# Cross attention with image tokens, batch 15: image-score copies and the small columns of six head pairs move from DVE to ACT

## What is computed

```
q, k, v     = heads(x @ W_q), heads(text @ W_k), heads(text @ W_v)
probs       = softmax(q k^T / sqrt(8))                  over 124 text tokens
text_out    = probs v
qsem        = l2norm(probs @ text)                      width 256
fused       = q k_ip^T / sqrt(8) + 0.5 * qsem . l2norm(image)     4 image tokens
ip_out      = (softmax(fused) * mask) v_ip
out         = (text_out + ip_out) @ W_out + b_out + x
```

## Time and profile before

| | |
|---|---|
| Median of 3 runs | 218.13 us (216.04 to 218.46) |
| Profiled execution, its own time | 217.86 us |
| Its span, first to last instruction | 215.8 us |
| Granted TensorE clock | 1.000 |
| PE busy | 204.6 us (95%) |
| DVE busy | 181.1 us (84%) |
| ACT busy | 169.1 us (78%) |
| POOL busy | 149.7 us (69%) |

### The profile page before, as it was taken

The page is one execution under the profiler, slowest core; times in us unless marked ns, Lnnn a source line. Parts: engine busy times, 40 slices in busy tenths (PEclk is TensorE's granted clock), DMA queues, the critical chain, the costliest instruction groups (busy, mean ns, idle before and its releaser), DMA issues.

```text
span 215.8 us, 6904 instructions
## 1 busy us (share of the span) xinstructions
PE 204.6 (95%) x1589; PEld 191.5 (89%) x1589; DVE 181.1 (84%) x1147; ACT 169.1 (78%) x554; POOL 149.7 (69%) x255
## 2 busy tenths in 40 slices
PE   8898959999997999999999999999999999998984
PEld 8777959999996999999999999999999999987973
DVE  4547758998977798997979797989979798989893
ACT  2639949897986888897988888888969888887721
POOL 2165007379794979879696969698796969697870
PEclk9999999999999999999999999999999999999999
DMA  5524443837364462747365554647364656433101
GB/s 132 146 83 105 109 122 64 225 77 237 58 174 122 120 185 56 208 109 210 95 186 122 163 140 130 170 88 213 68 205 100 189 120 171 94 92 103 46 5 46
DMA packets 41580, 27.45 MB, mean 127 GB/s; under 512 B 8513, under 2 KB 39898, under 8 KB 41562
## 3 DMA queue, kind: packets, MB, share of 16 engines
q1 hardware_dynamic: 40922, 26.81, 47.5%
q10 hardware_dynamic: 640, 0.43, 0.8%
HBM read 10.06 MB, written 1.43 MB: 53 GB/s over the span
## 4 chain that ended last, share of the span: by engine, by line
PE 77%; DVE 5%; POOL 4%; DMA 4%; SPq 4%; ACT 3%; issue 2%; POOLq 0%; DVEq 0%
PE main_ps L974 14%; PE main_ps L976 14%; PE probsT_ps L956 13%; PE pa L946 9%; PE score_ps L1010 7%; DMA k_split<-kip_d 4%; PE pb L1038 4%; PE pb L1050 3%; PE pa L1066 3%; SPq L385 2%; PE main_ps L891 2%; PE pa L1058 2%; POOL rnorm L511 2%; PE pa L886 2%; DVE junk L734 2%
## 5 line engine op out<-in xcount | busy, mean ns | idle before, releaser
L629 ACT ACTIVATE probs<-score_ps,negmax 128x124 f32<-128x124 f32 x320 | 92.5, 401 | 2.0 <-DVE negmax L799 1.9
L734 DVE CUSTOM_DVE_ANT_0 junk<-main_ps,probs 128x124 f32<-128x124 f32 x320 | 77.8, 280 | 2.3 <-PE main_ps L976 2.1
L974 PE MATMUL main_ps<-main_rhs,probsT 124*128 124x137 f32 x320 | 64.2, 281 | 0.7 <-DVE small L736 0.6
L976 PE MATMUL main_ps<-main_rhs,probsT 124*128 124x137 f32 x320 | 63.3, 279 | 0.0
L511 POOL TENSOR_TENSOR rnorm<-clamped,exponent 128x20 f32<-128x20 f32 x15 | 53.2, 3545 | 1.1 <-DVE clamped L719 1.1
L799 DVE TENSOR_REDUCE negmax<-score_ps 128x4 f32<-128x496 f32 x80 | 53.1, 663 | 0.0
L597 ACT ACTIVATE probsT<-probsT_ps 124x512 f32<-124x512 f32 x80 | 49.8, 622 | 3.4 <-PE probsT_ps L956 3.2
L974 PEld LDWEIGHTS main_ps<-main_rhs,probsT 124*128 124x128 f32 x320 | 49.0, 190 | 1.7 <-issue 1.3
L976 PEld LDWEIGHTS main_ps<-main_rhs,probsT 124*128 124x128 f32 x320 | 48.7, 188 | 0.0
L956 PE MATMUL probsT_ps<-ident_sb,probs 128*124 128x128 f32 x320 | 47.9, 272 | 0.0
L956 PEld LDWEIGHTS probsT_ps<-ident_sb,probs 128*124 128x124 f32 x320 | 38.4, 139 | 5.9
(11 more groups left out here) (162 smaller groups left out, 319.2 us busy)
## 6 DMA issues: line engine op xcount, KB each, us to landing
main_rhs<-g_stage SPq DMA_DIRECT2D x16, 660.0 KB, 4.1
vrep<-vip_d SPq DMA_DIRECT2D x13, 320.0 KB, 3.5
k_diag<-k_stack SPq DMA_DIRECT2D x60, 48.0 KB, 2.2
ctxT_sb<-ctxT SPq DMA_DIRECT2D x16, 124.0 KB, 2.7
k_diag<-k_stack SPq DMA_DIRECT2D x60, 32.0 KB, 2.0
xT_sb<-xT SPq DMA_DIRECT2D x16, 80.0 KB, 2.1
xn_sb<-xn SPq DMA_DIRECT2D x15, 80.0 KB, 2.0
out<-out_sb SPq DMA_DIRECT2D x15, 80.0 KB, 3.5
```

The lines of the kernel that those rows point to most:

```text
L629: last = act.activation(probs[p][:, h, :], score_ps[(p * G + g) % 2][:, j * TOK:j * TOK + T], ACT.Exp, bias=negmax[p][:, h:h + 1])
L734: dve.tensor_tensor_reduce(junk[:, 2 * r + a, :], u, probs[wb][:, h, :], 1.0, 0.0, ALU.mult, ALU.add, norm2[wb][:, h:h + 1])
L974: pe.matmul(main_ps[r][:, 0:MAIN], probsT[mp][:, 2 * r, :], blk[:, RW - MAIN:RW], start=True, stop=True)
L976: pe.matmul(main_ps[r][:, MAIN:2 * MAIN], probsT[mp][:, 2 * r + 1, :], blk[:, 0:MAIN], start=True, stop=True).then_inc(s_main, 1)
```

## The change

**Part 1.** In the window of batch 15, DVE no longer copies the image scores. For each of the five groups ACT does it, behind its wait for the maximum and ahead of the four exps, and counts in `s_tail_ip`. The sum of L857 waits for all five.

**Part 2.** At the end, `norms` of groups 1, 2 and 3 becomes `squares(0)` to `squares(2)`: the same sums of squares without the copy, with `s_tail_squares` counted once for each pair. ACT's `small_copied(k)` waits for it, copies the 26 columns of pair 2 + k, and increments `s_norm`. The norms of group 4 stay with DVE.

```diff
@@ ACT, window, in each group @@
                         act.wait_ge(s_max, grp + 1)
+                        if w == B - 1:
+                            sc = score_ps[(p * G + g) % 2][:, :].rearrange("s (h t) -> s h t", t=TOK)
+                            act.activation(ip_score[p][:, HG * g:HG * g + HG, :], sc[:, :, T:TOK], ACT.Copy).then_inc(s_tail_ip, 1)
                         for j in range(HG):
@@ ACT, behind the windows @@
             act.wait_ge(s_tail_fill, TAIL)
+            def small_copied(k):
+
+                act.wait_ge(s_tail_squares, k + 1)
+                act.activation(small[1][:, PG + k, :], main_ps[k % 2][:, T:T + SMALL], ACT.Copy).then_inc(s_norm, 1)
+
             transposed(B * G - 2, 0)
+            small_copied(0)
+            small_copied(1)
             act.wait_ge(s_tail_tr, 1)
             turned(0, 0, 3, pa)
+            small_copied(2)
             transposed(B * G - 1, 1)
+            small_copied(3)
+            small_copied(4)
+            small_copied(5)
             act.wait_ge(s_tail_centred, 1)
@@ DVE, window, in each group @@
-                        dve.tensor_copy(ip_score[p][:, HG * g:HG * g + HG, :], sc[:, :, T:TOK])
+                        if w != B - 1:
+                            dve.tensor_copy(ip_score[p][:, HG * g:HG * g + HG, :], sc[:, :, T:TOK])
@@ DVE, behind the windows @@
-            norms(B, 0, 0)
-            norms(B, 0, 1)
+            def squares(g):
+
+                for r in range(PG):
+                    pair = (B * G + g) * PG + r - 4 * PG
+                    dve.wait_ge(s_norm, pair - 1)
+                    dve.wait_ge(s_main, pair + 1)
+                    for a in range(2):
+                        h = HG * (g + 1) + 2 * r + a
+                        u = main_ps[r][:, a * (T + SMALL):a * (T + SMALL) + T]
+                        last = dve.tensor_tensor_reduce(junk[:, 2 * r + a, :], u, probs[1][:, h, :], 1.0, 0.0, ALU.mult,
+                                                        ALU.add, norm2[1][:, h:h + 1])
+                    last.then_inc(s_tail_squares, 1)
+
+            squares(0)
+            squares(1)
             dve.wait_ge(s_norm, NPAIR * (B - 1) + PG * PARTED[1])
             stats(1, PARTED[0], PARTED[1], tiles, s_tail_stats, 0)
-            norms(B, 0, 2)
+            squares(2)
...
+            dve.wait_ge(s_norm, NPAIR * B - PG)
             norms(B, 0, 3)
...
             dve.wait_ge(s_fuse, 2 * (B - 1) + 1)
+            dve.wait_ge(s_tail_ip, G)
             dve.tensor_tensor(tail_fused[:, :, :], tail_fused[:, :, :], ip_score[1][:, :, :], ALU.add).then_inc(s_fuse, 1)
```

More of the change, by code:

```diff
@@ L185, in xattn_program @@
         s_tail_fill = sem("s_tail_fill")
+        s_tail_squares = sem("s_tail_squares")
+        s_tail_ip = sem("s_tail_ip")
         s_vipT_mm = sem("s_vipT_mm")
```

## The result

| | before | after |
|---|---|---|
| Median of 20 runs | 217.06 us (215.93 to 218.97) | 218.59 us (217.24 to 220.11) |
| Ratio to before, 95% interval | | 1.0061 (1.0038 to 1.0085) |
| Span of the profiled execution | 215.8 us | 216.3 us |
| Stretch from the attention sum of batch 15 to the end of the last addition | 16.95 us | 18.36 us |

The kernel became slower by 0.6%, 1.3 us by the ratio; the two medians lie 1.5 us apart. The forecast was 219.1 us, +1.25 us on the profiled execution, as the likeliest case.

The account below looks back on a forecast made before the run. TensorE was taken as full up to the last window, then DVE's chain from 203.47. A 0.99 stall, plus 0.43 up to the first statistics, less 0.17 at the second, gave +1.25: 217.86 to 219.1 us, range 217.4 to 220.5.

Parts of the forecast that it names:

- The score copies: Batch 15's five image-score copies moved to ACT: worth about nothing, group 4's exps beginning at 201.95 instead of 201.97.
- Step (a): ACT's queue: pair 2's copy stands behind four exps and a probabilities' copy, starting at 203.43, done at 203.62.
- Step (b): From ACT's end to TensorE 0.06: pair 4's product starts at 203.68 instead of 202.69, a stall of 0.99.
- Steps (c) and (d): Pair 4's squares 0.85 behind its product; pair 5's copy, queued behind group 4's probabilities' copy (205.33 to 205.81), ends at 206.00.
- Step (e): DVE's first statistics wait for ACT's copies: 206.03 instead of 204.61, 1.42 late; pair 6's squares at 206.49.
- Step (f): Pair 7's squares at 206.91; the second statistics wait for its copy: 207.66 instead of 206.41, 1.25 late.
- Step (g): From the second statistics on, order as before; POOL's powers just in time, 0.18 to spare, adding nothing.
- The ScalarE rule: Skill page's activation cost, 186 ns and 0.833 ns a column: 0.21 for ACT's 26-column copy, making the sum 0.06 more, 219.2.
- The DRAIN rule: DVE's next op waits for an empty pipeline: each removed copy worth 0.18, gain 0.72, against 0.10 and 0.40 by the chain.
- one stall only: Rival: pair 4's wait comes once, later handoffs hidden, removed copies give 0.40 back: +0.59, 218.5; chance 0.15.
- Not slower: Rival: ACT's copies come in time, only DVE's removed copies count, no more than about 0.33 gained: 217.5; chance 0.08.
- Dear handoffs: Rival: ACT's copies of pairs 2, 5, 7 each cost 0.31 more with handoffs, 0.93 added: 220.1 or more; chance 0.10.

Follow-up runs that it names:

- Part 1 alone: The kernel before, with only the five image-score copies of batch 15 moved from DVE to ACT: stretch 16.98 us, ratio 1.0002.
- Pair 5 ahead of that copy: The change, with ACT's copy of pair 5 ahead of its copy of group 4's probabilities: stretch 18.14 us, ratio 1.0088.
- the kernel with both places mended: The change, with pairs 2 and 3 copied by DVE and pair 5's copy ahead of group 4's probabilities: stretch 16.96 us, ratio 1.0011.
- the best kernel here: The kernel before, with the small columns of pairs 6 and 8 alone copied by ACT: stretch 16.75 us, ratio 0.9989.
- the run with four of them left: The change, with the copies of pairs 2 and 3 kept on DVE, pairs 4 to 7 on ACT: stretch 17.18 us, ratio 0.9995.
- part 2 alone: The change, with the image-score copies given back to DVE: stretch 18.64 us in both executions, ratio 1.0076.

## Why the prediction was right

The times of after are set 0.89 later here, to stand on the scale of before.

- **The score copies, about nothing:** right. The exps were forecast at 201.95 and came at 201.97. The copy lasts 0.17 to 0.22, and holds the exps 0.06 to 0.08, for which I took 0.07. Part 1 alone shows the rest.
- **Step (a), place in the queue:** right to the hundredth, pair 2's copy at 203.43.
- **Step (b), stall of 0.99:** the mechanism is right, the handoff was mis-sized. From ACT's end to TensorE I took 0.06, from a row on another bank and another wait. Pair 4's product started 0.19 behind the copy's end (if the first of the two copies at 202.54 takes 0.19 like the lone ones), and pair 8's 0.15 (206.15 and 0.19, then 206.49). Pair 7's, though, started 0.05 behind pair 5's copy (205.06 and 0.19, then 205.30), so the handoff has no one price, and what sets it is not shown. Pair 4's came at 203.81 and not 203.68. The profile's 0.95 of idle counts from the end of the product before, at 201.97; against its old start the product is 1.12 late, where I had 0.99.
- **Steps (c) and (d):** 0.85 to the first square (202.92 to 203.77) is as taken. Step (d) says 0.94 from the product to group 4's transposes, but its 204.69 is 1.01 behind 203.68; the slip is in the text, and the trace has 1.01 (202.92 to 203.93). The 0.13 of step (b) is handed on: ACT's second probabilities' copy 205.46 instead of 205.33, pair 5's copy done 206.14 instead of 206.00. Pair 5 ahead of that copy gives back the share that was put down to the queue.
- **Step (e):** first statistics 1.56 late, forecast 1.42. Pair 6 came at 206.50 (206.49), since DVE starts it 0.33 behind the statistics, not the 0.46 of before, which held some waiting for TensorE.
- **Step (f):** second statistics 1.42 late, forecast 1.25. Pair 7's square came at 207.07 instead of 206.91, behind its late product. What is given back between the two statistics, 0.17 forecast and 0.14 measured, is the size of the pause that the kernel before has there (0.18) and the change has not. The forecast timed pair 7 by its product, 0.42 behind pair 6, and did not ask why it had been 0.70 before. That this came near is in part luck; with no pause in before the change would cost about 1.6 (an estimate).
- **Step (g):** right. POOL had 0.21 to spare ahead of the third power, forecast 0.18. From the second statistics on nothing was lost or won.
- **The sum:** +1.25 forecast, +1.41 on the stretch, 1.3 by the ratio. The term that was too small is the handoff from ACT to TensorE. The 219.1 itself lies 0.5 above the median of after for another reason: it starts from one execution of 217.86, and the median of before is 217.06.
- **The ScalarE rule.** An estimate of 0.21 for a copy of 26 columns, by the Trainium skill's page "ScalarE: Activation LUTs", section "What ACT_TABLE_LOAD costs": the four copies that stand alone took 0.19 each, as by the line through this kernel's rows. The measurement decides for 0.19.
- **The DRAIN rule.** A copy of 0.18 would be worth its whole length by the Trainium skill's page "VectorE: DVE Perf Modes", section "The DRAIN you can't avoid". Two copies less gave 0.20, 0.10 each, so the trace does not agree with that. The same paragraph adds that a next op that is not held starts earlier, and with this the trace agrees; the prediction left it out.

Of the rivals, *one stall only* is wrong on its second half: after the stall the removed copies do not come back, as the kernel with both places mended shows. *Not slower* was wrong on its price too: with the queue in order the stretch is that of before, not 0.33 shorter, and the best kernel here is 0.20 shorter. *Dear handoffs* is ruled out by the lone copies at 0.19 and by the run with four of them left.

## What to carry to other kernels

Moving a small operation to an idle engine puts it in that engine's queue: look at what stands ahead of it at the moment its input is ready, not at the engine's share of busy time. Here two copies of 0.19 us cost 1.2 us because they released a bank that TensorE was about to need, and DVE's squares waited behind it. And an operation that someone waits for at once gains nothing by moving even into an empty queue; move the one behind which the first engine still has other work.

## What was not expected of the hardware

**The clock at the end.** The granted clock of the last stretch was 0.89 in the profile of after. By the microsecond:

```profile
213.00:214.00 1.00, 0.54 (x2) 0.30 (x2) 0.10 (x1) 0.27 (x1) 0.00 (x0) 1.00 0.25 74
214.00:215.00 1.00, 0.00 (x0) 0.00 (x0) 0.22 (x1) 0.00 (x0) 0.00 (x0) 0.93 0.03 8
215.00:216.00 1.00, 0.00 (x0) 0.00 (x0) 0.00 (x0) 0.00 (x0) 0.00 (x0) 0.50 0.26 82
```

It fell to 0.50, the lower of TensorE's two levels (1.2 GHz), only after the last product, which ran from 213.32 to 213.86 at full speed. In the second execution of part 2 alone it stayed at 1.00 through 217, so the fall differs between executions. At the end it touches no product and cost nothing.

**The clock early in the run.** In three of the eleven profiled executions (the second ones of the change and of part 2 alone, and that of pairs 6 and 8) the clock was at 0.50 from 32 to 34 us as well, with TensorE busy all the time. Part 2 alone has one execution without this fall and one with it. The same two main products of 124x137 took 0.40 us without it (at 31.85) and 0.67 with it (at 32.26).

The two executions were 0.04 apart at a maximum of DVE (31.70 and 31.74) and 1.81 apart at the attention sum of batch 15 (195.31 and 197.12), and their stretch is the same. So the fall costs about 1.8 us of time, shifts the end, and changes nothing in it. Ahead of it TensorE had waited 2.00 for a DMA, up to 30.73; the execution without it had waited 2.09, up to 30.82, so what brings the fall stays open.

**Pauses of DVE that have no releaser.** Part 2 alone has its gap ahead of pair 7's second square in both executions, and the change has it in neither. It is not alone: part 1 alone pauses at the same square, which starts 0.43 behind the first. The kernel before pauses one pair earlier. The read of pair 6's second square comes 0.32 behind that square, where 0.20 to 0.21 is usual:

```profile
205.28 0.28 DVE L734 CUSTOM_DVE_ANT_0 junk<-main_ps,probs 128x124 f32<-128x124 f32 x1
205.60 0.08 DVE L734 DVE_READ_ACCUMULATOR2_ANT norm<- 128x1 f32 x1
```

With the copy behind it, 0.49 pass from that square to pair 7's (205.28 to 205.77), against 0.31 one group earlier (203.68 to 203.99): the 0.18 of pause. The kernel with pairs 6 and 8 on ACT pauses at the same read. The profile names no releaser, and nothing here tells what the pauses are; moving a few instructions of ACT or DVE was enough to bring them or take them away.
